# Turns through TensorE as two halves, scatters interleaved, and another order in attention, in a four-layer graph kernel

## The reference

```
L0: q, k, v = h @ w{q,k,v}.T + b;  q2, k2, v2 = (q, k, v) @ wi{q,k,v}.T + bi   (16 heads of 64)
    mask[src, dst] = softplus(type weight) where there is an edge, -inf elsewhere, a value on the diagonal
    attn = softmax(q2 @ k2.T * scale + mask);  y = (attn @ v2) @ wo.T + bo
L1: u = h @ root + bias + sum over 8 relations r of (mean of h[src] over edges of type r) @ weight[r]
    z = [u, h] @ w_gate + b_gate;  y = tanh(u) * z + h * (1 - z)
L2: two layers  h @ W_self + (mean of h[src] over all edges) @ W_neigh + b, relu after the first
L3: W[row, col] += edge weight;  y = h @ W.T + bias
```

## Time and profile before

| | us |
|---|---|
| three runs | 937.17, 942.64, 937.59 |
| median | 937.59 |
| profiled execution | 937.65 |
| its span, first to last instruction | 935.9 |
| TensorE busy | 913.5 (98%) |
| VectorE busy | 610.6 (65%) |
| GpSimd busy | 489.6 (52%) |
| ScalarE busy | 361.9 (39%) |

### The profile page before, as it was taken

How to read it: one execution, slowest core, us unless ns; L and a number is a source line. 1 busy time by engine, 2 the same in 40 slices (tenths; PEclk the granted TensorE clock), 3 DMA queues, 4 the chain that set the end, 5 groups by cost and what they waited for, 6 DMA issues and landing times.

```text
span 935.9 us, 13614 instructions
## 1 busy us (share of the span) xinstructions
PE 913.5 (98%) x4723; PEld 802.7 (86%) x4723; DVE 610.6 (65%) x1003; ACT 361.9 (39%) x568; POOL 489.6 (52%) x436
## 2 busy tenths in 40 slices
PE   5999999998999999999999999999999999999998
PEld 4999999997788887888888888888888888887886
DVE  6998888885886735656656565665646656434645
ACT  6433333344886334232223232323224345233532
POOL 5334444456676454757576575757685601320363
PEclk9999999999999999999999999999999999999999
DMA  8998756571337617453445535344333444333412
GB/s 204 243 278 223 228 155 154 153 195 2 52 43 206 161 20 257 110 171 98 142 114 167 150 113 157 104 149 113 92 110 122 157 130 136 118 107 90 136 45 90
DMA packets 89907, 128.60 MB, mean 137 GB/s; under 512 B 34480, under 2 KB 67456, under 8 KB 89856
## 3 DMA queue, kind: packets, MB, share of 16 engines
q1 hardware_dynamic: 72784, 123.54, 43.4%
q0 software_dynamic: 15552, 0.11, 4.2%
q10 hardware_dynamic: 1520, 4.30, 1.4%
HBM read 117.17 MB, written 7.59 MB: 133 GB/s over the span
## 4 chain that ended last, share of the span: by engine, by line
PE 89%; DMA 3%; DVE 3%; POOL 2%; issue 1%; ACT 1%; POOLq 0%; DVEq 0%; ACTq 0%
PE ps L672 47%; PE ps L471 18%; PE ps L746 8%; PE ps L515 4%; PE ps L635 4%; PE ps L595 2%; PE ps L551 2%; PE ps L538 2%; DMA raw<-in_L_gnn_weight 1%; DMA weight_d<-weight_sum,cell 1%; DVE wlo_all L1372 1%; DMA b_in<-in_L_gnn_biv 1%; PE ps L432 1%; POOL weight_d L1863 1%; POOL mean_lo L1842 1%
## 5 line engine op out<-in xcount | busy, mean ns | idle before, releaser
L1372 DVE TENSOR_TENSOR wlo_all<-raw,whi_all 128x1024 fp32r<-128x1024 f32 x120 | 199.3, 1669 | 121.6 <-ACT whi_all L960 121.5
L471 PE MATMUL ps<-acts,whi_all 128*128 128x384 f32 (+1 forms) x640 | 164.2, 337 | 0.0
L1842 POOL TENSOR_TENSOR mean_lo<-mean_f,mean_hi 128x384 fp32r<-128x384 f32 x76 | 88.6, 1165 | 119.6 <-ACT mean_hi L1110 119.3
L1110 ACT ACTIVATE mean_hi<-mean_f 128x384 fp32r<-128x384 f32 x76 | 39.9, 526 | 272.8 <-DVE mean_f L1539 272.8
L672 PE MATMUL ps<-whi_all,mean_hi 128*128 128x512 f32 x452 | 139.7, 390 | 2.5 <-POOL mean_lo L1842 2.5
L672 PE MATMUL ps<-wlo_all,mean_hi 128*128 128x512 f32 x452 | 139.3, 389 | 0.0
L672 PE MATMUL ps<-whi_all,mean_lo 128*128 128x512 f32 x452 | 139.2, 389 | 0.0
L960 ACT ACTIVATE whi_all<-raw 128x1024 fp32r<-128x1024 f32 x120 | 124.5, 1049 | 24.5 <-PE ps L672 18.0
L471 PEld LDWEIGHTS ps<-acts,whi_all 128*128 128x128 f32 x640 | 117.0, 190 | 0.1
L1863 POOL DMA_INDIRECT weight_d<-weight_sum,cell x48 | 95.5, 1989 | 31.5 <-DMA weight_d<-weight_sum,cell 18.6
L1810 POOL DMA_INDIRECT count_d<-met,cell x48 | 77.6, 1617 | 60.0 <-DMA count_d<-met,cell 46.8
(11 more groups left out here) (209 smaller groups left out, 1718.6 us busy)
## 6 DMA issues: line engine op xcount, KB each, us to landing
raw<-in_L_gnn_weight SPq DMA_DIRECT2D x64, 512.0 KB
rows_b<-rows_d SPq DMA_DIRECT2D x24, 384.0 KB, 5.2
raw<-in_L_gnn_w_gate SPq DMA_DIRECT2D x16, 512.0 KB
raw<-in_L_gnn_W_self SPq DMA_DIRECT2D x16, 512.0 KB
raw<-in_L_gnn_W_neigh SPq DMA_DIRECT2D x16, 512.0 KB
count_d<-total_r SPq DMA_DIRECT2D x8, 576.0 KB
rel_r<-count_d SPq DMA_DIRECT2D x8, 576.0 KB, 4.5
raw<-in_L_gnn_wq SPq DMA_DIRECT2D x32, 128.0 KB
```

What stands on the lines that cost most here:

```text
L471: mm = pe.matmul(ps[:, j % 2, 0:N], stationary[j % RING][:, k, :], acts[:, a, moving, k, :], start=i == 0, stop=i == 3 * KT - 1)
L1110: act.activation(mean_of(q, k, 0)[:, 0, :], sums_of(q, k), ACT.Copy).then_inc(S["mean_hi"], 1)
L1372: dve.tensor_tensor(wlo_row[slot], raw[slot][:, :], whi_row[slot].bitcast(F32), ALU.subtract)\
L1842: pool.tensor_tensor(mean_of(q, k, 1)[:, 0, :], sums_of(q, k), mean_of(q, k, 0)[:, 0, :].bitcast(F32), ALU.subtract).then_inc(S["mean_lo"], 1)
```

## The change

1. A turn of features or of the output weight is done as two turns of 64 rows each (`ROWS`), the first into one bank and the second into the next. Each turn now uses both banks 6 and 7, so it waits for `turn_lo` of the turn before. The readers take both banks in runs of 64 columns. Turns of probabilities and sums stay as they are.
2. GpSimd issues mask scatters 0 to 31 alone, and then two mask scatters ahead of every two counts until the masks are done (in the first eight rounds). The six `pair_low` stand behind counts 35, 37, 39, 43, 45 and 47.
3. The planes of the first relation are added up ahead of the rows' low halves.
4. In attention, scores and output turns come ahead of the turns of the even head; turn 2 of the odd head comes behind the weighing of the even one; maxima, exps, inversions and halves are put in another order to match. The last meets are placed elsewhere within the value step, and the first pair's low halves ahead of its inversions.

```diff
@@ -209,7 +210,8 @@
         S_CREDIT = 2
-        PAIR_AFTER = (17, 19, 21, 25, 27, 29)
+        PAIR_AFTER = (35, 37, 39, 43, 45, 47)
+        MASK_ALONE = 2 * EC // 3
@@ -263,6 +265,18 @@
             return mean[a][:, i:i + 1, :] if i < 2 else rel_r[:, 0, 1 + a:2 + a, :]
+
+        def turned_blocks(n):
+
+            return ps[:, 6:8, 0:ROWS * n].rearrange("p f (b n) -> p b f n", n=ROWS)
+
+        def in_halves(blocks):
+
+            return blocks.rearrange("p b (f n) -> p b f n", f=2)
+
+        def in_blocks(row):
+
+            return row.rearrange("p (b f n) -> p b f n", f=2, n=ROWS)
@@ -424,21 +438,25 @@
+            HALF_ROWS = (slice(0, ROWS), slice(ROWS, P))
+
             def turn(y, source, f):
-                need(pe, S["turn_lo"], y - 1)
+                need(pe, S["turn_lo"], y)
                 for nt in range(NT):
-                    mm = pe.transpose(ps[:, 6 + y % 2, P * nt:P * nt + P],
-                                      source[:, nt, P * f:P * f + P], ident[:, :])
+                    for i, rows in enumerate(HALF_ROWS):
+                        mm = pe.transpose(ps[:, 6 + i, ROWS * nt:ROWS * nt + ROWS],
+                                          source[rows, nt, P * f:P * f + P], ident[rows, rows])
                 mm.then_inc(S["turned"], 1)
...
-                need(pe, S["turn_lo"], y - 1)
+                need(pe, S["turn_lo"], y)
                 for k in range(blocks):
-                    mm = pe.transpose(ps[:, 6 + y % 2, P * k:P * k + P],
-                                      source[:, nt, P * k:P * k + P], ident[:, :])
+                    for i, rows in enumerate(HALF_ROWS):
+                        mm = pe.transpose(ps[:, 6 + i, ROWS * k:ROWS * k + ROWS],
+                                          source[rows, nt, P * k:P * k + P], ident[rows, rows])
                 mm.then_inc(S["turned"], 1)
@@ -456,8 +474,10 @@
                 for k in range(KT):
-                    mm = pe.transpose(ps[:, WO_BANK[j] + k // 4, P * (k % 4):P * (k % 4) + P],
-                                      raw[j % RING][:, P * k:P * k + P], ident[:, :])
+                    for f in range(2):
+                        rows = slice(ROWS * f, ROWS * f + ROWS)
+                        mm = pe.transpose(ps[:, WO_BANK[j] + f, ROWS * k:ROWS * k + ROWS],
+                                          raw[j % RING][rows, P * k:P * k + P], ident[rows, rows])
                 mm.then_inc(S["weight_turned"], 1)
@@ -599,30 +619,29 @@
             for pair in range(H // 2):
                 e, o = 2 * pair, 2 * pair + 1
-                if pair:
-                    turn_probs(e, 0)
-                    turn_probs(e, 1)
                 if pair and o + 1 < H:
                     scores(pair + 1, 0)
                 if o + 1 < H:
                     scores(pair + 1, 1)
-                if o + 1 == H:
+                else:
                     turn_output(0)
                     turn_output(1)
                 if pair:
+                    turn_probs(e, 0)
+                    turn_probs(e, 1)
                     weigh_values(e - 1)
                 turn_probs(e, 2)
-                turn_probs(o, 0)
                 spread_sums(pair)
                 if o + 1 < H:
                     scores(pair + 1, 2)
                 else:
                     turn_output(2)
+                turn_probs(o, 0)
                 turn_probs(o, 1)
-                turn_probs(o, 2)
                 if o + 1 == H:
                     turn_output(3)
                 weigh_values(e)
+                turn_probs(o, 2)
             weigh_values(H - 1)
             def output_blocks(f, nt, blocks):
@@ -907,13 +926,12 @@
                 act.wait_ge(S["turned"], y + 1)
-                act.activation(target, ps[:, 6 + y % 2, 0:N], ACT.Copy).then_inc(S["turn_hi"], 1)
+                act.activation(in_blocks(target), turned_blocks(NT), ACT.Copy).then_inc(S["turn_hi"], 1)
...
                 act.wait_ge(S["turned"], y + 1)
-                act.activation(h_t[0][:, 0:blocks, P * nt:P * nt + P],
-                               ps[:, 6 + y % 2, 0:P * blocks].rearrange("p (k n) -> p k n", n=P), ACT.Copy)\
+                act.activation(in_halves(h_t[0][:, 0:blocks, P * nt:P * nt + P]), turned_blocks(blocks), ACT.Copy)\
                    .then_inc(S["turn_hi"], 1)
@@ -949,8 +967,9 @@
                 b = WO_BANK[j]
-                act.activation(whi[j][:, :, :] if j < RING else wo_t[0][:, j - RING, :, :],
-                               ps[:, b:b + 2, :].rearrange("p b (k n) -> p (b k) n", n=P), ACT.Copy)\
+                target = whi[j] if j < RING else wo_t[0][:, j - RING, :, :]
+                act.activation(target.rearrange("p k (f n) -> p k f n", f=2),
+                               ps[:, b:b + 2, :].rearrange("p f (k n) -> p k f n", n=ROWS), ACT.Copy)\
                    .then_inc(S["w_hi"], 1)
@@ -1056,27 +1075,28 @@
                 if pair and more:
                     exp(e + 2, 0)
                     exp(o + 2, 0)
+                if not more:
+                    column_high(0)
+                probs_high(e, 2)
                 if more:
                     exp(e + 2, 1)
+                    exp(o + 2, 1)
                 else:
-                    column_high(0)
                     column_high(1)
-                probs_high(e, 2)
                 probs_high(o, 0)
                 if more:
-                    exp(o + 2, 1)
+                    exp(e + 2, 2)
                 else:
                     column_high(2)
                 probs_high(o, 1)
+                if more:
+                    exp(o + 2, 2)
+                else:
+                    column_high(3)
                 probs_high(o, 2)
-                if not more:
-                    column_high(3)
-                if more:
-                    exp(e + 2, 2)
-                    exp(o + 2, 2)
-                read_spread(pair)
                 if pair:
                     pair_high(pair - 1)
+                read_spread(pair)
             act.wait_ge(S["probs_turned"], H * NT)
             act.dma_start(xres[:, :, :], x.rearrange("(t p) d -> p t d", p=P)).then_inc(S["x_in"], 16)
@@ -1302,15 +1322,16 @@
                 dve.wait_ge(S["turn_hi"], y + 1)
-                dve.tensor_tensor(target, ps[:, 6 + y % 2, 0:N], hi.bitcast(F32), ALU.subtract).then_inc(S["turn_lo"], 1)
+                dve.tensor_tensor(in_blocks(target), turned_blocks(NT), in_blocks(hi).bitcast(F32), ALU.subtract)\
+                   .then_inc(S["turn_lo"], 1)
...
                 cols = slice(P * nt, P * nt + P)
-                dve.tensor_tensor(h_t[1][:, 0:blocks, cols],
-                                  ps[:, 6 + y % 2, 0:P * blocks].rearrange("p (k n) -> p k n", n=P),
-                                  h_t[0][:, 0:blocks, cols].bitcast(F32), ALU.subtract).then_inc(S["turn_lo"], 1)
+                dve.tensor_tensor(in_halves(h_t[1][:, 0:blocks, cols]), turned_blocks(blocks),
+                                  in_halves(h_t[0][:, 0:blocks, cols]).bitcast(F32), ALU.subtract)\
+                   .then_inc(S["turn_lo"], 1)
@@ -1428,17 +1451,17 @@
                         score_max(1, n - 6)
-                    for n_met in range((1, 1, 2)[n % NT]):
+                    for n_met in range((2, 1, 1, 2, 1, 1, 2, 1, 1, 2, 2, 0)[n]):
                         meet(met_now)
...
                         score_max(3, 0)
+                probs_low(0, 0)
+                probs_low(0, 1)
                 invert_sums(0)
                 invert_sums(1)
-                probs_low(0, 0)
-                probs_low(0, 1)
@@ -1460,29 +1483,31 @@
                     score_max(e + 2, 1)
                 if pair:
                     probs_low(e, 0)
-                    probs_low(e, 1)
                 if more:
                     score_max(o + 2, 1)
+                if pair:
+                    probs_low(e, 1)
                 if not more:
                     column_low(0)
-                    column_low(1)
                 if pair:
                     make_pair(pair - 1)
                 probs_low(e, 2)
+                if more:
+                    score_max(e + 2, 2)
+                    score_max(o + 2, 2)
+                else:
+                    column_low(1)
                 probs_low(o, 0)
                 if more:
-                    score_max(e + 2, 2)
+                    invert_sums(e + 2)
                 else:
                     column_low(2)
                 probs_low(o, 1)
                 if more:
-                    score_max(o + 2, 2)
+                    invert_sums(o + 2)
+                else:
+                    column_low(3)
                 probs_low(o, 2)
-                if not more:
-                    column_low(3)
-                if more:
-                    invert_sums(e + 2)
-                    invert_sums(o + 2)
             def last_pair_low(pair):
                 dve.wait_ge(S["pair_hi"], pair + 1)
@@ -1817,8 +1842,9 @@
```

(18 more changed lines are left out.)

## The result

The changed kernel takes 963.99 us (median of four runs, 960.72 to 966.86) against 937.38 for the kernel before beside it: ratio 1.027, 95% interval 1.024 to 1.030. It is slower. I had predicted 951 with a range of 932 to 960. The profiled execution took 966.86 us, with a span of 965.1: 29.2 more than before.

The account below looks back on a forecast made before the run. TensorE, busy 98% of the span, was taken as the bound; from 937.65 us, +8.3 output start, +2.1 restart, +4.9 turns, +0.2 buffer, -2.2 wait and -0.4 end turns gave +12.9, about 951 us, range 932 to 960.

Parts of the forecast that it names:

- TensorE's own arrival: End of attention: the new queue order makes TensorE ready for the output step at 290.5 in place of 295.47.
- The mechanism: Output step: it waits for pair_low, queued behind later counts and ending at 303.7, 13 us behind TensorE; start +8.3 us.
- The step that failed: GpSimd's interleaved scatters: eight rounds at 6.2 us, 49.6, plus 5.2 for cells, so count 15 ends at 197.4.
- the upper bound: Output step's latest start: 312 us (+16.5), with a slow landing beside weight loads and some 2 us scatters.
- The landing ahead of count 16: GpSimd after count 15: a landing of 2.3 us plus 3.8 for loads beside it; count 16 starts at 203.5.
- Counts 16 to 47: GpSimd's later counts: 5.81 us a pair without pair_low, 6.91 with one; count 46 starts at 297.3.
- Restart: TensorE resuming at the output step after 13 us of rest: slower at first, +2.1 us.
- The mask: Before attention's first maximum: last mask scatter ends near 193.5, mask loaded near 204, before 208.8; costs nothing, bound 2 us.
- Turns in halves: Turns of features and output weight: n blocks cost 0.345 + 0.057n us against 0.109n, +4.3 us in all.
- The rival of half loads at full price: Turns in halves: a pair's loads take 0.11 us, so blocks gain nothing; +8.5, 959.5 us, chance 0.09.
- the +0.2 for the shared banks: Turns using both banks: each waits for the low half of the one before, +0.2 us at the tightest tiles.
- The 2.2 us wait: First relation: TensorE's wait for a mean's last half goes, as counts end 40 us sooner; -2.2 us.

Follow-up runs that it names:

- e1: The changed kernel with pair_low placed behind counts 25, 27, 29, 31, 33 and 35; 934.26 us, ratio 0.996.
- e2: The changed kernel with pair_low placed behind counts 29, 31, 33, 37, 39 and 41; 941.99 us, ratio 1.005.
- e5: The kernel before with only GpSimd's order changed: interleaved scatters and pair_low behind counts 35 to 47; 962.45 us, ratio 1.028.
- e4: The kernel before with only the queue order of attention changed; 933.06 us, ratio 0.995.
- e10: The changed kernel with all 48 mask scatters ahead of the counts again, pair_low still behind counts 35 to 47; 980.64 us in one run.
- e6: The changed kernel with pair_low placed as in e1 and features turned whole, only the output weight in halves; 930.10 us, ratio 0.992.
- e11: The changed kernel with ScalarE writing zeros for VectorE's low halves of the q, k and v weight blocks (all but the first); 954.79 us, ratio 1.019.
- e7: The changed kernel with pair_low placed as in e1, and both features and output weight turned whole; 931.34 us, ratio 0.993.
- e3: The kernel before with only the turns of features and of the output weight done as halves; 939.50 us, ratio 1.0022.
- e8: e6 with scatters and pair_low in the order of the kernel before; 933.86 us, ratio 0.997.
- e9: The changed kernel with VectorE's low halves of the q, k and v weight blocks written as zeros by a memset; 963.65 us in one run.

## Why the prediction was wrong, point by point

**TensorE's own arrival: right.** Ready at 290.8 + 0.2 against 290.5. A pair of attention takes 7.73 us (`pair_high` at 240.12 and, five pairs on, at 278.75) against 7.8.

**The mechanism: right.** `pair_low` behind counts 35 to 47 ends after TensorE's arrival. e1, e2 and e5 show it. I had taken 13 us for the wait, and it was 30.5. One reading in that sum was loose: 6.91 is an average over seven pairs of counts of which six have a `pair_low`, and the five that I priced with it hold four; that moves the sum by less than 0.5 us.

**The step that failed** is "eight rounds of two mask and two count scatters ... 6.2 a round, 49.6" with cells 5.2, "count 15 ends at 197.4". It ended at 211.5. Of those 14.1 us, 3.1 are a later start: mask 32 began at 145.7 here, and elsewhere between 142.3 and 145.7, but for 137.1 in e4, though GpSimd's order up to there is the same in all; I didn't follow that up. The other 11.0 lie in the rounds, 65.8 against 54.8: masks 20.1 in place of 15.4, counts 28.1 in place of 24.6, cells with the gaps around them 6.9 in place of 5.2, and the remaining idle 10.7 in place of 9.6. I had priced every scatter at its bare length, 0.96 and 1.54, although a long one stood in the earlier trace rows; I kept "some 2 us scatters" for the upper bound. That bound was too low as well: 312 against 321.6.

Why bare lengths failed: VectorE writes low halves of weight blocks for 0.30 of the time from 20 us to 208 us, and the scatters begin inside one at about that rate, with or without interleaving. Before, 18 of the 53 scatters of this stretch did; after, 16 of 62, and in the rounds 10 of 32 (over the other traces it varies, from 10 of 54 in e10 to 20 of 62 in e6). So these traces don't show that the interleaving made a collision more likely. It moved counts 5 to 13, which before came behind the last low half, into the stretch where low halves are written. My 1.54 was read at 241.71, behind that stretch. The rows of the stretch itself had the price: before, masks 32 to 47 took 17.3 us together, and the five counts that were issued by 208 took 1.68, 2.21, 1.89, 2.08 and 2.08, a mean of 1.99. By these, my estimate for 16 masks and 16 counts is 17.3 + 31.8 = 49.1, which is 9 us over the bare 40.0; measured are 48.2, 8.2 over. In e11, which takes the low half off VectorE, 6.6 of the 8.2 us of extra length are gone.

**The landing ahead of count 16:** 7.26 against my 6.16, +1.1. Its reason, the loads beside it, was not tested.

**Counts 16 to 47: close.** 98.9 us from the start of 16 to that of 47; I had 203.5 to about 299, 96. About 2 of the +3 are the landing ahead of 298.02, which cost 4.42 us of idle where 2.3 is usual, beside the output weight's loads. The stretch's row (span, busy of PE, PEld, DVE, ACT and POOL, clock, DMA share, GB/s):

```profile
287.00:298.00 11.00, 2.89 (x17) 2.30 (x15) 4.24 (x7) 3.65 (x7) 5.58 (x4) 0.85 0.75 275
```

In e11 the landings near there cost 1.7 us at most. That the loads make a landing slow was not tested. With GpSimd on the path, its own scatter becomes the kernel's: the times of the late kernels spread by 6 to 12 us. The one comparison that traces allow is e5 (957.77), whose GpSimd has the same order and ends its last `pair_low` at 314.13, 7.4 us sooner: 2.9 of that is the earlier start of mask 32, 1.2 the rounds, 0.7 the landing ahead of count 16, and 2.6 counts 16 to 47.

**Restart: right.** Rows of two stretches after, columns as above, answer to the earlier trace rows:

```profile
321.60:325.60 4.00, 3.98 (x10) 3.17 (x11) 0.00 (x0) 0.00 (x0) 0.00 (x0) 0.52 0.02 4
325.60:330.00 4.40, 4.40 (x33) 3.39 (x32) 0.44 (x1) 1.03 (x1) 0.00 (x0) 1.00 0.10 18
```

The granted clock is 0.52, the level of 1.2 GHz, after 30 us without matmuls, and full 4 us later. The eighteenth matmul of the step starts 5.80 us after the first, against 3.90 before: 1.9 lost, where I had 2.1.

**The mask: right for TensorE only.** I had the last mask scatter near 193.5 and the mask loaded near 204, ahead of the first maximum. The last one ended at 207.7, for the same reason as the counts of the rounds, and VectorE waited 4.3 us; it cost TensorE nothing that shows, as said above.

**Turns in halves: right in mechanism, a little dear.** A gate round is 736.15 - 731.50 = 4.65 against 4.46: +0.19, as worked out. The drain shows at the return; these are TensorE's rows around one turn, and the loads of its six half turns:

```profile
736.15 0.27 PEld L449 LDWEIGHTS ps<-ident,u 64*128 64x128 f32 x6 [0.35 <-issue]
736.15 0.40 PE L449 MATMUL ps<-ident,u 64*128 64x64 f32 x6
736.49 0.72 PE L691 MATMUL ps<-whi_all,h_t_hi 128*128 128x512 f32 x2
```

The second pair starts 0.108 after the first and each later one 0.06, where I took 0.057 for all. With the 0.32 between two starts going in, 0.15 coming back and 0.106 for the load, a group of n blocks in halves costs 0.33 + 0.06n, against my 0.345 + 0.057n. The rival of half loads at full price fell with that: loads of two pairs start 0.06 apart. The Trainium skill ("TensorEngine Tiling (Array Packing)", Key Properties) warns that a change of tiling mode drains the engine, and the return in these rows agrees. The same page of the Trainium skill, under Theoretical Speedup, gives up to twice the speed; 0.06 a block against 0.11 comes near to that, but only within a group. In sum I had +5.6 for features and -1.3 for the output weight; e1, e6 and e7 gave +4.2 and -1.2. Why features cost 1.4 less than the sum of their groups is open, and the +0.2 for the shared banks was not measured by itself. (The outer bound of +12.8 should read 13.1, 4.3 + 169 x 0.052.)

**The 2.2 us wait: gone, and the way I said, but it was cheaper to lose.** In the changed kernel the counts are done 29 us sooner than before and the wait is 0.3. e3, which leaves the scatters alone, has 0.3 as well. In its profiled execution count 47 starts at 344.63 in place of 347.03, the relations' tables are asked for at 347.8 in place of 350.1, and the mean's low half starts at 369.41 in place of 370.89; TensorE, slowed by the halves, comes 0.9 us later. Together that covers the 2.2. So 2.4 us of luck in when the counts end are enough, with that, to lose this wait, and the forecast's -2.2 can't be booked under the scatters alone.

**Sum.** Forecast 950.6, measured 966.9 in the profiled execution: +17.8 for the start of the output step (321.6 against 303.8), -1.5 for all that follows (3.1 against 4.6). At the median the miss is 13.

## What to carry to other kernels

Before an operation moves behind others in an in-order queue, work out when its last reader comes to want it, and leave a margin as wide as the queue's scatter from run to run (6 to 12 us here), for once the queue is late every slow landing is paid in full. When items of a queue are moved to another stretch of the kernel, price them by rows of that stretch and not by their bare length: what they meet there on the other engines sets it (here 1.99 us for a count beside VectorE's low halves and 1.54 behind them). Half-height turns in threes and fours cost more by the change of tile shape than the shorter stream gives (4.2 us in sum); in groups of eight and sixteen they gained (1.2 us).

## What the runs showed of the hardware

- An indirect DMA that GpSimd begins while VectorE runs a 128x1024 subtraction with both inputs in SBUF (1.18 us) is lengthened by about the rest of it: up to 2.00 us for a mask in place of 0.97, up to 2.56 for a count in place of 1.56. With the operation on ScalarE (e11) none was. The Trainium skill ("SBUF — State Buffer", Who interferes with whom) has VectorE and GpSimd share a pair of SBUF ports under an exclusive lock, and says that a VectorE instruction with two SBUF inputs contends with a GpSimd instruction that reads SBUF; the lengths here agree. The same section of the Trainium skill reports a probe in which `tensor_tensor` did not stall DMAs, and on that the runs here differ.
- The 128x256 `scalar_tensor_tensor` of the meets on VectorE (0.47 us, both tensors in SBUF) does the same on its scale. Most masks that begin in one are longer than 0.96 by what is left of it less about 0.13: by 0.18 with 0.31 left (141.20 after), by 0.23 with 0.37 left (169.87 in e8). A few are longer by all of it (0.38 with 0.38 left, 90.69 in e4), and those that begin in its first 0.02 us are not longer (82.58 before).
- A memset of 128x1024 on VectorE (0.91 us) lengthens such a DMA as well: 2.35 for a count in place of 1.56, 1.85 for a mask in place of 0.97 (e9).
- A change of tile shape cost 0.09 us each way in the gate step: going in 0.32 between two starts where the stream is 0.23, coming back 0.15 where it is 0.06. The load of the first full matmul was not hidden and cost 0.106 more.
- After 11 us without a matmul (e2) the first four microseconds ran at a granted clock of 0.50, and after 45 (e10) at 0.61. From its first matmul the twentieth of the output step started 7.29 us later in e2 and 6.74 in e10, against 5.23 before: the longer rest was no dearer.
